# Token MLP on two 64-row tiles of the array: products split in halves, hidden blocks taken in pairs

## The reference

```python
h = _ln(x, ln1_g, ln1_b)
h = afno2d(h, w1, b1, w2, b2)
h = h + residual
residual = h
m = _ln(h, ln2_g, ln2_b)
m = _gelu(m @ mlp_w1 + mlp_b1) @ mlp_w2 + mlp_b2
return m + residual
```

## Time and profile before

| | |
|---|---|
| median of three runs | 2095.67 us |
| the profiled execution | 2094.48 us |
| its span, first to last instruction | 2092.7 us |
| TensorE busy | 1934.5 us (92%) |
| VectorE, ScalarE, GpSimd busy | 1164.2, 1011.5, 432.4 us |
| mean granted TensorE clock | 0.975 |
| the MLP on TensorE | about 660 to 1480 us of the span |

### The profile page before, as it was taken

The page is one execution under the profiler, slowest core; times in us unless marked ns, Lnnn a source line. Parts: engine busy times, 40 slices in busy tenths (PEclk is TensorE's granted clock), DMA queues, the critical chain, the costliest instruction groups (busy, mean ns, idle before and its releaser), DMA issues.

```text
span 2092.7 us, 68971 instructions
## 1 busy us (share of the span) xinstructions
PE 1934.5 (92%) x31104; PEld 1581.5 (76%) x31104; DVE 1164.2 (56%) x2480; ACT 1011.5 (48%) x1644; POOL 432.4 (21%) x425
## 2 busy tenths in 40 slices
PE   4999995688898999999999999999899999999997
PEld 4777762566665999999999999999677777777774
DVE  3687887956755433333333333332366767666675
ACT  3765545566664333333333333333466666655652
POOL 3212103955531000000111000000321211211200
PEclk9999996799999999999999999999999999999999
DMA  9425728306336111111111111114722565457214
GB/s 162 98 48 83 127 57 140 59 4 119 74 99 152 31 31 31 31 30 30 30 30 30 30 30 30 30 30 73 107 37 51 96 112 98 74 86 127 56 38 95
DMA packets 299701, 141.05 MB, mean 67 GB/s; under 512 B 275760, under 2 KB 298032, under 8 KB 299440
## 3 DMA queue, kind: packets, MB, share of 16 engines
q1 hardware_dynamic: 299440, 137.08, 35.6%
HBM read 74.14 MB, written 62.91 MB: 65 GB/s over the span
## 4 chain that ended last, share of the span: by engine, by line
PE 77%; DVE 10%; ACT 3%; SPq 3%; issue 3%; POOL 2%; DMA 1%; DVEq 0%; POOLq 0%; ACTq 0%
PE ps L688 19%; PE ps L673 19%; PE ps L523 8%; PE ps L586 8%; PE ps L537 7%; PE ps L602 6%; PE ps L555 4%; PE ps L504 4%; DVE u L919 3%; DVE st L956 2%; SPq L357 1%; DVE xs L944 1%; DVE xn L976 1%; PE ps L565 1%; ACT z L727 1%
## 5 line engine op out<-in xcount | busy, mean ns | idle before, releaser
L1068 DVE TENSOR_TENSOR gl<-g,gh 128x512 fp32r<-128x512 f32 x192 | 156.8, 816 | 476.4 <-ACT gh L854 476.4
L919 DVE TENSOR_TENSOR u<-ps,clamp 64x192 f32<-64x192 f32 (+1 forms) x864 | 377.6, 437 | 27.7
L851 ACT ACTIVATE g<-ps,colp 128x512 f32<-128x512 f32 x192 | 132.3, 689 | 529.2 <-PE ps L673 529.2
L523 PEld LDWEIGHTS ps<-const,z 128*48 128x48 f32 x8384 | 265.0, 124 | 115.7 <-issue 106.2
L727 ACT ACTIVATE z<-ps 64x512 f32<-64x512 f32 x366 | 234.3, 640 | 115.8 <-PE ps L504 108.8
L523 PE MATMUL ps<-const,z 128*48 128x64 f32 (+1 forms) x8384 | 269.4, 217 | 12.2 <-issue 7.3
L1155 POOL COPY xn<-xs 128x512 f32<-128x512 f32 x144 | 151.1, 1086 | 552.5 <-PE ps L504 360.3
L688 PE MATMUL ps<-w2h,gh 128*128 128x384 f32 x768 | 261.9, 341 | 0.0
L688 PE MATMUL ps<-w2h,gl 128*128 128x384 f32 x768 | 258.6, 337 | 0.0
L688 PE MATMUL ps<-w2l,gh 128*128 128x384 f32 x768 | 257.5, 335 | 0.0
L537 PE MATMUL ps<-zf,w 112*64 112x512 f32 (+2 forms) x992 | 246.7, 572 | 5.1 <-ACT zf L747 1.3
(11 more groups left out here) (70 smaller groups left out, 2446.9 us busy)
## 6 DMA issues: line engine op xcount, KB each, us to landing
after<-xs SPq DMA_DIRECT2D x96, 384.0 KB, 5.4
xs<-after SPq DMA_DIRECT2D x94, 384.0 KB, 8.8
after<-om SPq DMA_DIRECT2D x32, 384.0 KB, 4.3
out<-xs SPq DMA_DIRECT2D x32, 384.0 KB, 5.5
xm<-after SPq DMA_DIRECT2D x30, 384.0 KB, 6.3
xs<-in_x SPq DMA_DIRECT2D x24, 384.0 KB, 8.0
wstage<-in_spectral SPq DMA_DIRECT2D x16, 210.0 KB, 5.8
xs<-in_x SPq DMA_DIRECT2D x4, 768.0 KB, 11.8
```

Of the source, the lines that this page charges most:

```text
L523: mm = pe.matmul(ps[a * SIDE:a * SIDE + BLOCK, F2_BANK, n * L.kh:(n + 1) * L.kh], z[:, g % 2, slot, :], basis(col + a * SIDE, L.kh), start ...
L919: dve.tensor_tensor(u[to, g % 2, :, start + b:start + size:BATCH], whole, limited, ALU.subtract).then_inc(u_ready, 1)
L1068: dve.tensor_tensor(gl[:, n % 4, :], g[:, n % 2, :], gh[:, n % 4, :], ALU.subtract).then_inc(g_low, 1)
```

## The change

Every matmul of the two products is cut into two of 64 rows, one on rows 0 to 63 and one on rows 64 to 127, issued one behind the other. The two halves of one sum must not go to the same bank at the same time. So the hidden blocks are taken in pairs `p`: in part 0 the upper rows work on the first block's bank and the lower rows on the second's, and in part 1 the banks are exchanged. Both banks are complete only after part 1. `second` does the same with output banks 0/1 against 2/3. Each part still has 9 or 12 steps, now of two matmuls.

```diff
+        MM2_ORDER = (0, 2, 1, 3)
...
+        mm1_half, mm2_half = sem("mm1_half"), sem("mm2_half")
...
             def token_mlp():
-                def first(r, i, n):
-                    if n == 0:
-                        pe.wait_ge(mt_low, KC * (r + 1) + i * (2 * KC))
-                    if n >= 2:
-                        pe.wait_ge(g_ready, HC * r + n - 1 + i * (2 * HC))
...
+                def first(r, i, p, part):
+
+                    if part:
+                        pe.wait_ge(mm1_half, HC // 2 * r + p + 1 + i * HC)
+                    else:
+                        if p:
+                            pe.wait_ge(g_ready, HC * r + 2 * p + i * (2 * HC))
+                        else:
+                            pe.wait_ge(mt_low, KC * (r + 1) + i * (2 * KC))
...
                     for k in range(KC):
-                        at = slice(k * HIDDEN + n * P, k * HIDDEN + (n + 1) * P)
                         for m, (a, b) in enumerate([(w1h, mth), (w1h, mtl), (w1l, mth)]):
-                            mm = pe.matmul(ps[:, MM1_BANKS[n % 2], :], a[:, at], b[r][:, k, :],
-                                           start=k == 0 and m == 0, stop=k == KC - 1 and m == 2)
-                    mm.then_inc(mm1_done, 1)
...
+                            for half in range(2):
+                                rows, n = slice(half * SIDE, (half + 1) * SIDE), half ^ part
+                                at = k * HIDDEN + (2 * p + n) * P
+                                mm = pe.matmul(ps[:, MM1_BANKS[n], :], a[rows, at:at + P], b[r][rows, k, :],
+                                               start=part == 0 and k == 0 and m == 0,
+                                               stop=part == 1 and k == KC - 1 and m == 2)
+                    mm.then_inc(mm1_done if part else mm1_half, 1)
+
+                def second(r, i, p, part):
+
+                    swapped = (p + part) % 2
+                    if part:
+                        pe.wait_ge(mm2_half, HC // 2 * r + p + 1 + i * HC)
+                    else:
+                        pe.wait_ge(g_low, HC * r + 2 * p + 2 + i * (2 * HC))
...
+                        if p == 0:
+                            wait_past(pe, om_ready, 4 * r + i * 8)
+                    for n in range(2 * p, 2 * p + 2):
+                        at = slice(n * CHANNELS, (n + 1) * CHANNELS)
+                        for s in range(2):
+                            for m, (a, b) in enumerate([(gh, w2h), (gh, w2l), (gl, w2h)]):
+                                for half in range(2):
+                                    rows, j = slice(half * SIDE, (half + 1) * SIDE), 2 * (half ^ swapped) + s
+                                    mm = pe.matmul(ps[:, MM2_BANKS[j], 0:CHANNELS], a[rows, n % 4, j * P:(j + 1) * P],
+                                                   b[rows, at], start=n == 0 and part == 0 and m == 0,
+                                                   stop=n == HC - 1 and part == 1 and m == 2)
...
+                    if part == 0:
+                        mm.then_inc(mm2_half, 1)
 
                 def tile(r, i, following):
                     for t in range(HC + LAG):
                         if t < HC:
-                            first(r, i, t)
+                            first(r, i, t // 2, t % 2)
                         if 0 <= t - TURN_AT < KC and following:
                             turn(*following, t - TURN_AT)
                         if t >= LAG:
-                            second(r, i, t - LAG)
+                            second(r, i, t // 2 - 1, t % 2)
...
                 def first(r, i, n):
-                    act.wait_ge(mm1_done, HC * r + n + 1 + i * (2 * HC))
+                    act.wait_ge(mm1_done, HC // 2 * r + n // 2 + 1 + i * HC)
```

More of the change, by code:

```diff
@@ L662, in token_mlp @@
             def token_mlp():
-                def first(r, i, n):
-                    if n == 0:
-                        pe.wait_ge(mt_low, KC * (r + 1) + i * (2 * KC))
-                    if n >= 2:
-                        pe.wait_ge(g_ready, HC * r + n - 1 + i * (2 * HC))
-                    if r == 0 and first_of(i):
-                        pe.wait_ge(w1_low, n + 1)
+                def first(r, i, p, part):
[6 more added lines that the diff above has]
+                            pe.wait_ge(mt_low, KC * (r + 1) + i * (2 * KC))
+                        if r == 0 and first_of(i):
+                            pe.wait_ge(w1_low, 2 * p + 2)
@@ new lines, in first @@
+                    mm.then_inc(mm1_done if part else mm1_half, 1)
[5 more added lines that the diff above has]
+                        pe.wait_ge(g_low, HC * r + 2 * p + 2 + i * (2 * HC))
+                        if r == 0 and first_of(i):
+                            pe.wait_ge(w2_low, 2 * p + 2)
+                        if p == 0:
[9 more added lines that the diff above has]
+                                                   stop=n == HC - 1 and part == 1 and m == 2)
+                                    if n == HC - 1 and part == 1 and m == 2:
+                                        mm.then_inc(mm2_done, 1)
+                    if part == 0:
+                        mm.then_inc(mm2_half, 1)
@@ L1073, in results @@
                     wait_past(dve, m_stored[r], i * (16 * BATCH))
-                    for j in range(4):
-                        dve.wait_ge(mm2_done, 4 * r + j + 1 + i * 8)
+                    for n, j in enumerate(MM2_ORDER):
+                        dve.wait_ge(mm2_done, 4 * r + n + 1 + i * 8)
                         dve.tensor_tensor(om[:, r, j, :], ps[:, MM2_BANKS[j], 0:CHANNELS], xm[:, r, j, :],
```

## The result

The changed kernel takes 2239.8 us (median of 4, 2235.2 to 2248.7), the kernel before on the same chip 2094.4 (2093.1 to 2100.7). The ratio is 1.0694, with a 95% interval from 1.0664 to 1.0724: 7% slower, where the forecast was 2245 and 7%. The profiled execution took 2248.7 us, the longest of the four.

What follows compares the result with a forecast made beforehand. It took TensorE's own steps to bound the MLP, so every wait is added whole: 2094.5 us plus 122.6 of waits plus 27 of clock made 2244, stated as 2245, 7% slower; range 2185 to 2305.

Steps and rivals of the forecast that it cites:

- The steps: MLP products: two 64-row matmuls take as long as one 128-row step, 231 ns in `first` and 175 in `second`.
- shorter steps: Rival, chance 0.20: MLP steps shrink to 213 and 160 ns, 51 us gained; time 2194, or 2167 if the clock holds.
- in turn: Rival, chance 0.06: the two halves run one after the other, so the MLP products double; time 2960.
- not slower: Rival, chance 0.03: 64-row matmuls much cheaper; decides from steps of 182 and 126 ns down, 2045 at 165 and 110.
- Pair 1: Tile's start: TensorE waits for both Gelus with no `second` between, 2.42 us each, 38.7 in 16 tiles.
- pairs 2 to 4: Within a tile: a `second` stands between, leaving a wait for both Gelus of 0.32 us, 48 times, 15.4 us.
- the tile's end: Last pair's `second` waits for `gl` of both blocks: 2.5 us, 1.7 in the last tile, 39.2 in all.
- pair 5: ScalarE empties a turn before the second Gelu: 0.67 us added in 15 tiles, 0.32 in the last, 10.4 in all.
- Half waits: Waits on the half before, bare only at a tile's start (`mm1_half`) and end (`mm2_half`): 0.31 us each, 9.9 in all.
- Turns: Transposes on all 128 rows force shape changes around turns 0 and 2: 0.30 us a turn, 30 turns, 9.0 us.
- The tile: One MLP tile grows from 51.4 us by 7.7 to 59 before any clock spell.
- The clock: MLP: half of 32 long TensorE gaps bring a 3.6 us spell at 1.2 GHz, 1.7 us lost each, 27 us.

Runs made afterwards that it cites:

- e4: The kernel before, its order and no pairs, with only the second product in 64-row halves that rotate over the four output banks: 2172.1 us, ratio 1.0333.
- e2: The changed kernel with half-row matmuls whose results nobody reads put in front of each tile's two long waits: 2213.3 us, ratio 1.0549.
- e6: The changed kernel with TensorE's loop over the MLP's tiles written out, nothing else: 2240.2 us, ratio 1.0675.
- e1: The changed kernel with pair order and release by pairs kept, but 128-row matmuls and no waits on the half before: 2208.3 us, ratio 1.0524.
- e9: e8 with VectorE's statistics and normalising back in their old places, whole 128-row matmuls: 2117.7 us, ratio 1.008.
- e10: e9 with the products on two 64-row tiles, TensorE's loop kept: 2157.7 us, ratio 1.0279.
- e3: The changed kernel with the last pair's `second` moved behind the next tile's first parts: 2173.8 us, ratio 1.0366.
- e7: e3 with the turns one step earlier (VectorE's statistics moved along) and TensorE's tile loop written out: 2207.9 us, ratio 1.0527.
- e8: e7's order with the loop kept, whole 128-row matmuls and no waits on the half before: 2171.2 us, ratio 1.0328.
- e5: The kernel before with both MLP products on rows 0 to 63 only, half of every sum left out: 2806.5 us, ratio 1.3382.

## Why the forecast held, step by step

- **The steps** (231 and 175 ns). Exact: without a wait, 2081 ns for nine and 2106 for twelve, in both kernels. From start to start, in the timeline of the changed kernel:

```profile
1219.37 0.41 PE L681 MATMUL ps<-mth,w1h 64*128 64x512 f32 x2
1219.59 0.42 PE L681 MATMUL ps<-mtl,w1h 64*128 64x512 f32 x2
1219.83 0.42 PE L681 MATMUL ps<-mth,w1l 64*128 64x512 f32 x2
1220.06 0.41 PE L681 MATMUL ps<-mth,w1h 64*128 64x512 f32 x2
```

  Four starts stand 0.23 apart on average, two halves each. The rivals "shorter steps", "in turn" and "not slower" fall here. The rule of the Trainium skill ("TensorE: Matmul & The Clock Gate", "The mechanism") that a weight load overlaps only on other rows would have shown as a shorter step; it doesn't, as the earlier trace rows said. The same section also lets a load run ahead into a background weight buffer; that would fit these rows, though no run here shows the buffer.
- **Pair 1** (2.42 each). Measured 2.26. I added ScalarE's records end to end, but they overlap:

```profile
1211.12 0.39 PE L681 MATMUL ps<-mth,w1l 64*128 64x512 f32 x2
1211.55 0.69 ACT L869 ACTIVATE g<-ps,colp 128x512 f32<-128x512 f32 x1 [11.61 <-PE ps L681]
1212.27 0.63 ACT L872 ACTIVATE gh<-g 128x512 fp32r<-128x512 f32 x1
1212.80 0.67 ACT L869 ACTIVATE g<-ps,colp 128x512 f32<-128x512 f32 x1
1213.52 0.50 PE L681 MATMUL ps<-mth,w1h 64*128 64x512 f32 x2 [2.02 <-ACT g L869]
```

  The rounding starts at 1212.27 with 0.63, the second Gelu at 1212.80, 0.10 before the first would end. The earlier trace rows have only the other change, from a Gelu to a rounding, where 0.03 lies between. The same excess explains pairs 2 to 4 (0.32, measured 0.18), and helps to explain the tile's end (2.5, measured 2.24) and pair 5 (0.67, measured 0.41).
- **Half waits** (0.31 each): 0.33 and 0.38.
- **Turns** (0.30 each): 0.33, in the chain as 0.59 for 0.44 and 2.28 for 2.10. The total is right, its parts are luck. From start to start, the change ahead of the transposes costs the 0.10 that line 504 gave, the one behind them 0.17 (the next matmul starts 0.20 after the last transpose, 0.03 before), and the transposes themselves 0.06. The bare load on the way back, 0.10 in the sum, adds only 0.02: the earlier trace rows are from the kernel before, which already pays for it. The Trainium skill ("TensorEngine Tiling (Array Packing)", "Key Properties") has the array drain at such a change. The traces fit that, with a next matmul that overlaps the last record by 0.07 us instead of 0.16 (e4), though record ends are modelled; the full 0.39 of a record, the prediction's bound, is not paid.
- **The tile.** Forecast 51.4 + 7.7 = 59.1; measured 58.4 to 58.5 without a spell, so 7.1. Over 16 tiles 113 us for the 122.6 in the sum: 9 too much.
- **The clock** (27 us, half of the gaps). 16 spells for 32 gaps, 1.5 us each; e2 took them away and won 27. "Half" was chosen between two rows and had luck on its side: e6, with the same gaps, had 21 spells. Without spells the prediction named 2217; e2 came to 2213.
- **What the sum lacked.** The jump back of TensorE's loop: 9.8 us, five waits of about 2 us. It nearly cancels the excess of 9 above, so the total is better than its parts.
- **The rest.** Outside the MLP the profiled execution is 8 us longer than before's. It is the longest of four that spread over 13 us, and the median is 9 below it, so nothing is read from that.

So the loss lies in waits that the pairing opens, in the clock spells behind them, in changes of shape and in the jump of the longer loop, and none of it in the length of a step. e1 and e9 show the waits with whole matmuls, e2 the clock, e4 and e10 the changes of shape, e6 the jump.

## What to carry to other kernels

Where TensorE is busy all the time and its steps are on all rows, as here, splitting them by rows shortens nothing; count then what the split asks of the order, above all which results must be complete at once and what stands between them and their reader. A gap of 2 us costs its own length and, in 16 to 21 of 32 cases here, 1.5 more in clock, so that work nobody reads can pay for itself (e2). When a step is moved by a constant, look for all that hangs on it, and at what each of these waits for (e3, e7, e8).

## What the runs showed of the chip

- **A TensorE that never idles can stay at the lower clock.** With 64-row matmuls on one half alone the granted clock was 0.50 through 1480 us in which TensorE was never idle (e5); with two halves side by side it is 1.00 (e2). Busy time alone doesn't tell the clock; why it stayed low is not shown, and no run has the one half at full clock.
- **The columns are the whole step at 1.2 GHz and not at 2.4.** 427 and 320 ns (e5, and e1's whole matmuls in its spells) are exactly 512 and 384 columns; 231 and 175 at full clock are 18 and 15 ns more than columns. What adds these at the higher level stays open.
- **A long loop body costs a wait at its jump.** The body of two tiles has twice the matmuls. The first and the last pair of tiles stand outside the loop, so it jumps back five times, and all five jumps show a wait of 1.7 to 2.1 us, in the trace from 902.5, 1021.6, 1144.8, 1268.4 and 1390.5. In e4, with 1.6 times the matmuls, they are 2.6 to 3.3; e1 with as many as before has none, and neither has e6 without the jump. The queue that brings instructions moved more as well, in the page's rows (packets, MB, share), of before and of after:

```profile
q8 instruction: 224, 3.67, 0.7%
```
```profile
q8 instruction: 286, 4.69, 0.9%
```

  That fetching the code again is the cause is inferred from these, not shown; e6, which moved 4.52 MB, also has more than before and no such wait.
- **Equal gaps don't all drop the clock.** 16 of 32 in the changed kernel and 21 spells in e6 with the same waits; the executions of the two spread over 13 and 15 us, those of the kernel before over 9 at most.

Not tried: the transposes of the turns on 64 rows, which would spare the changes of shape around them.
